# Penalty and maximum of the attention scores: one combined VectorE instruction per head in place of an addition and a reduction per eight heads

## What is computed

```
q, k, v = heads(norm(x) @ Wq.T + bq), heads(ctx @ Wk.T + bk), heads(ctx @ Wv.T + bv)
scores = einsum('bhqd,bhkd->bhqk', q / sqrt(16), k)
scores = scores + ((1.0 - attention_mask) * -10000.0)[:, None, :, :]
probs = softmax(scores, axis=-1)
x = x + tanh(g) * einsum('bhqk,bhkd->bhqd', probs, v)
```

## Time and profile before

| what | before |
|---|---|
| median of 3 runs | 851.88 us (849.93 to 851.89) |
| the profiled execution | 849.4 us |
| its span | 847.6 us |
| the attention stage's scores to exponentials | 481.5 to 613.7 us |

### The profile page before, as it was taken

How to read it: one execution, slowest core, us unless ns; L and a number is a source line. 1 busy time by engine, 2 the same in 40 slices (tenths; PEclk the granted TensorE clock), 3 DMA queues, 4 the chain that set the end, 5 groups by cost and what they waited for, 6 DMA issues and landing times.

```text
span 847.6 us, 15310 instructions
## 1 busy us (share of the span) xinstructions
PE 776.9 (92%) x5406; PEld 625.7 (74%) x5406; DVE 506.0 (60%) x1159; ACT 399.9 (47%) x817; POOL 227.0 (27%) x208
## 2 busy tenths in 40 slices
PE   8667899999999999999999789996789999999997
PEld 7466487788887888888887455654568878888886
DVE  5588875465583333343342897978766665756644
ACT  5598554244462222222223688778635344243222
POOL 0079210046501332232234166764300000000000
PEclk9989999999999999999999999999999999999999
DMA  8478740033242334443332600102004023050140
GB/s 303 143 263 300 279 169 1 1 126 125 99 164 69 63 63 70 78 79 63 68 45 31 221 13 27 63 2 75 2 2 102 1 51 76 1 126 0 27 100 26
DMA packets 37512, 74.47 MB, mean 88 GB/s; under 512 B 4448, under 2 KB 25568, under 8 KB 35680
## 3 DMA queue, kind: packets, MB, share of 16 engines
q1 hardware_dynamic: 30288, 64.16, 24.0%
q0 software_dynamic: 7152, 9.34, 6.4%
HBM read 59.76 MB, written 19.01 MB: 93 GB/s over the span
## 4 chain that ended last, share of the span: by engine, by line
PE 54%; DVE 16%; ACT 8%; DVEq 4%; issue 4%; DMA 2%; ACTq 0%; POOLq 0%; SPq 0%
PE t_y_ps L2281 8%; PE f_y L1775 4%; PE a_turned L999 3%; PE a_score L977 2%; ACT a_hhi L1165 2%; PE t_gate L2251 2%; PE a_score L978 2%; PE a_score L979 2%; PE t_up L2262 2%; PE t_up L2263 2%; PE t_up L2261 2%; PE t_gate L2252 2%; PE t_gate L2253 2%; PE a_proj L876 2%; PE t_h_turned L2270 2%
## 5 line engine op out<-in xcount | busy, mean ns | idle before, releaser
L2221 POOL DMA_INDIRECT sums<-t_y,t_dest x39 | 60.9, 1561 | 168.4 <-DMA sums<-t_y,t_dest 81.3
L2316 ACT CAST t_xT_hi<-t_x_turned 128x256 fp32r<-128x256 f32 x39 | 14.5, 372 | 139.2 <-PE t_x_turned L2242 139.2
L2281 PE MATMUL t_y_ps<-W,t_hidT 128*128 x312 | 73.8, 379 | 0.8 <-ACT t_hidT L2326 0.8
L1165 ACT CAST a_hhi<-a_hid 128x512 fp32r<-128x512 f32 x48 | 29.8, 620 | 87.5 <-DVEq L1450 85.9
L2281 PEld LDWEIGHTS t_y_ps<-W,t_hidT 128*128 128x128 f32 x312 | 59.1, 190 | 10.5 <-issue 1.0
L1452 DVE TENSOR_TENSOR a_hlo<-a_hid,a_hhi 128x512 fp32r<-128x512 f32 x48 | 33.2, 693 | 35.1 <-ACT a_hhi L1165 35.1
L1154 ACT ACTIVATE a_act_g<-a_score 128x512 f32<-128x512 f32 x48 | 28.6, 596 | 46.4 <-PE a_score L979 45.9
L2345 DVE TENSOR_TENSOR t_hid<-t_act_g,t_up 128x512 f32<-128x512 f32 x39 | 28.5, 731 | 35.9 <-ACT t_act_g L2321 32.6
L832 POOL TENSOR_TENSOR a_sc<-a_sc,a_nmx 128x512 f32<-128x512 f32 x32 | 33.3, 1042 | 55.8 <-DVE a_nmx L1298 55.8
L1114 ACT ACTIVATE a_pr<-a_sc,a_nmx 128x128 f32<-128x128 f32 x128 | 40.8, 390 | 14.3 <-DVE a_nmx L1298 13.5
L2356 DVE TENSOR_SCALAR t_y<-t_y_ps,t_dest 128x256 f32<-128x256 f32 x39 | 18.9, 484 | 38.3 <-PE t_y_ps L2281 38.3
(11 more groups left out here) (426 smaller groups left out, 2287.8 us busy)
## 6 DMA issues: line engine op xcount, KB each, us to landing
W<-in_w_dram SPq DMA_DIRECT2D x9, 1536.0 KB, 8.1
a_cb<-comb_rows SPq DMA_DIRECT2D x16, 512.0 KB, 8.2
W<-m_rows SPq DMA_DIRECT2D x14, 512.0 KB, 4.9
slot_tokens<-in_blank_rows_dram SPq DMA_DIRECT2D x1, 5031.0 KB, 20.5
t_x<-slot_tokens SPq DMA_DIRECT2D x39, 129.0 KB, 3.0
a_raw<-in_w_dram SPq DMA_DIRECT2D x3, 1536.0 KB, 6.7
X<-in_x_dram SPq DMA_DIRECT2D x4, 512.0 KB, 6.1
ctxT_all<-in_ctxT_dram SPq DMA_DIRECT2D x4, 512.0 KB, 8.7
```

Of the source, the lines that this page charges most:

```text
L1165: act.copy(hhi[u % 2][:], hid[u % 2]).then_inc(hhi_ready, 1)
L2221: pool.indirect_dma_start(sum_dram, bass.IndirectOffsetOnAxis(ap=dest[p][:, 0:1].bitcast(U32), axis=0), y[p][:], None, compute_op=ALU.add) ...
L2281: last = pe.matmul(y_ps[p][:, 0:D], hidT[p][:, h], W[:, ds(e, 1), at:at + D], start=(h == 0), stop=(h == HT - 1))
```

## The change

VectorE's `soft` becomes a loop over two groups of four heads. Each head is one `tensor_tensor_reduce`: it adds penalty and score, multiplies by -1 and writes the result to `sc`, and writes the smallest of the results to the head's column of `nmx`. The last of four signals `max_ready`, which now counts 4 a step, and `score_free` is gone: its waiters wait for the matching count of `max_ready`. The tile `sc` now holds the negated scores, so ScalarE's exponentials of groups 0 and 2 get a scale of -1, and POOL's `centre` subtracts `sc` from the broadcast `nmx`. The wait for old exponentials stands before each group in place of each half.

```diff
@@ block.sync
-                sp.wait_ge(score_free, 2 * CH * (c - 1))
+                sp.wait_ge(max_ready, 4 * CH * (c - 1))
@@ block.gpsimd, centre(s, g)
-                pool.wait_ge(max_ready, 2 * s + g // 2 + 1)
+                pool.wait_ge(max_ready, 4 * s + g + 1)
                 part = sc[s % 2][:, g]
-                pool.tensor_tensor(part, part, nmx[s % 2][:, g].rearrange("p (i o) -> p i o", o=1).broadcast_to([128, 4, 128]),
-                                   ALU.add).then_inc(centred_ready, 1)
+                pool.tensor_tensor(part, nmx[s % 2][:, g].rearrange("p (i o) -> p i o", o=1).broadcast_to([128, 4, 128]), part,
+                                   ALU.subtract).then_inc(centred_ready, 1)
@@ block.tensor, scores(s) and gate_up(u)
-                wait(pe, score_free, 2 * s)
+                wait(pe, max_ready, 4 * s)
...
-                    pe.wait_ge(score_free, 2 * B)
+                    pe.wait_ge(max_ready, 4 * B)
@@ block.scalar, exps(s, g)
-                    act.wait_ge(max_ready, 2 * s + g // 2 + 1)
+                    act.wait_ge(max_ready, 4 * s + g + 1)
                     for i in range(4):
-                        last = act.activation(pr[s % 2][:, g, i], sc[s % 2][:, g, i], ACT.Exp, bias=nmx[s % 2][:, g, i:i + 1])
+                        last = act.activation(pr[s % 2][:, g, i], sc[s % 2][:, g, i], ACT.Exp, bias=nmx[s % 2][:, g, i:i + 1],
+                                              scale=-1.0)
@@ block.vector, soft(s, half)
-                wait(dve, exp_ready, 4 * (s - 2) + 2 * half + 2)
-                part = sc[s % 2][:, 2 * half:2 * half + 2].rearrange("p r i t -> p (r i) t")
-                dve.tensor_tensor(part, score[:, half * 1024:(half + 1) * 1024].rearrange("p (h t) -> p h t", h=8),
-                                  pen[c % 2][:, j:j + 1].broadcast_to([128, 8, 128]), ALU.add).then_inc(score_free, 1)
-                dve.drain()
-                dve.tensor_reduce(nmx[s % 2][:, 2 * half:2 * half + 2].rearrange("p r i -> p (r i)"), part, AX.X, ALU.max,
-                                  negate=True).then_inc(max_ready, 1)
+                for r in (2 * half, 2 * half + 1):
+                    wait(dve, exp_ready, 4 * (s - 2) + r + 1)
+                    for i in range(4):
+                        last = dve.tensor_tensor_reduce(sc[s % 2][:, r, i], score[:, r * 512 + i * 128:r * 512 + (i + 1) * 128],
+                                                        pen[c % 2][:, j], -1.0, 3e38, ALU.add, ALU.min,
+                                                        nmx[s % 2][:, r, i:i + 1])
+                    last.then_inc(max_ready, 1)
```

More of the change, by code:

```diff
@@ L660, in attention_feed_forward @@
         proj_ready, kept_act, kept_dve, pen_ready = sem("proj_ready"), sem("kept_act"), sem("kept_dve"), sem("pen_ready")
-        score_ready, score_free, max_ready, exp_ready = sem("score_ready"), sem("score_free"), sem("max_ready"), sem("exp_ready")
+        score_ready, max_ready, exp_ready = sem("score_ready"), sem("max_ready"), sem("exp_ready")
         centred_ready = sem("centred_ready")
```

## The result

The changed kernel takes 844.02 us (median of 4 runs, 842.87 to 844.69), the kernel before 851.88 beside it (4 runs, 849.93 to 855.24): ratio 0.9888, 95% interval 0.9852 to 0.9924 (the two medians alone divide to 0.9908). The sign of the prediction holds. The gain is well over the 4.8 us forecast: 7.9 us by the medians, 9.5 by the ratio. The forecast's own range began at 844: the median is just inside it, while 851.9 x 0.9888 = 842.3 is outside, and just outside the wider range too, which began at 842.5. The profiled execution took 842.87 us with a span of 841.1.

The account below looks back on a forecast made before the run. The attention stage was taken as balanced, VectorE paying only where it is in the path. Terms: 1.4 + 0.5 + 1.0 + 2.2 - 0.3 = 4.8 us; 851.9 - 4.8 = 847.1 us; range 844 to 850.

Parts of the forecast that it names:

- the wider range: Total time: the 8 in 10 range, from 842.5 to 859 us.
- p = 0.275: VectorE's combined instructions: start-to-start pitch of 0.275 us, the maximum's write adding 0.075; a half 2.2 us, 0.24 less.
- rival 3: VectorE's combined instructions: the maximum comes for free, pitch 0.20, a half 1.6 us; 10.9 us gained, 841.0; chance 0.09.
- Rival 2: VectorE's combined instructions: no overlap, pitch 0.36, 6.7 us slower, 858.6; far end pitch 0.5, 883; chance 0.21 together.
- From 528 to 542: Within steps 5 to 9, VectorE fuller than TensorE: two of four halves counted, 2 x 0.24 = 0.5 us gained.
- steps 10 and 11: 561.7 to 579.7 us, VectorE doing one thing after another: four halves, 4 x 0.24 = 1.0 us gained.
- the late steps: Steps 12 to 15: 0.36 from exp 3 and 0.24 from the first half, three steps, plus 0.4: 2.2 us gained.
- gain 0.45 a step, it just fits: Steps 2 to 4: group 3's exponentials after 3.45 us instead of 3.9; three steps, 1.4 us gained.
- POOL's 9.17 of 10 leaves about 0.6 a step: Steps 2 to 4: POOL's busy share leaves about 0.6 us a step, enough for the 0.45 gain.
- The clock, left out of the sum: The lower granted clock after 580 us may move the time either way by a microsecond, held by the range.
- The later release of the score banks: Score banks freed by the last group's signal: steps 2 to 4 lose 0.3 us; covered in the full steps.

Follow-up runs that it names:

- the fourth of its traces: The changed kernel run again with no edit, as the control beside the reordering of POOL's queue: 842.84 us, ratio 0.9905 to the kernel before.
- the third: The changed kernel run again with no edit, as the zero for three variants beside it: 844.91 us, ratio 0.9893 to the kernel before.
- the two forms: The changed kernel with its signal per four heads, 847.22 us, and the same with one signal per half, 846.31 us.
- the old form with four signals: Kernel before, its addition and reduction split into four groups of 512 columns with a signal each: 859.39 us, ratio 1.0091.

## Why the prediction was right in sign and short in size

**The step that failed is the pitch, the term "p = 0.275" of "What takes its place".** The argument for it was half right. There is a second part, it lasts 0.083 us, and the Trainium skill's sentence ("VectorE: DVE Perf Modes", "Two Vector instructions with no wait between them") that an op that also writes its accumulator is two instructions agrees with the trace. The error was to add the part to the pitch instead of letting it run beside the next instruction. The pair of the earlier trace rows already showed it, with the line of the trace of before that stands between its two:

```profile
629.36 0.16 DVE L1405 MATCH_REPLACE8 a_oh<-a_largest,a_cur 128x16 f32<-128x16 f32 x1
```

The loads came 0.15 us apart while load and replacement last 0.09 and 0.16, so the replacement still ran when the next pair's load started. The pitch is 0.21, close to rival 3's 0.20, and rival 3 had been given 0.09. Rival 2 is refuted here: instructions of 0.286 and 0.083 us repeat every 0.21 us, and only where a drain was put in by hand did the pitch become 0.42.

The Trainium skill's rule that the next op doesn't start until the pipe is empty ("VectorE: DVE Perf Modes", "The DRAIN you can't avoid") does not hold for these instructions. The same section adds that a next op that isn't held starts earlier, which the prediction left out, and with that the trace agrees. The Trainium skill's advice not to fuse chained ops for speed and to keep the count of ops low (same page, "Rules for kernel authors") did not hold for this pair either: there are 448 more instructions, and the kernel is faster.

**With the measured pitch the forecast's own terms.** A half gets shorter by 2.44 - 1.69 = 0.75 us, not 0.24. From 528 to 542 two halves were counted: 1.5 us, and steps 5 to 9 gave 1.6. In steps 10 and 11 four halves would be 3.0, TensorE caps it as rival 3 said (2.0), and 1.8 came. In the late steps two halves and the wait were to count; 4.1 us for three steps and 1.0 in the last, 5.1 against 6.1 of rival 3. These terms were rightly placed, and too small because of the pitch. In the late steps the clock may have a share as well: the changed kernel took 23.2 us for steps 12 to 14 and 8.9 to the last exponential where the clock from 580 to 610 was 1.00 (the fourth of its traces), and 24.6 and 10.3 where it was 0.89 (the third), the level of before. Against before that is a gain of 5.8 or of 3.1 us.

**The early steps, "gain 0.45 a step, it just fits", failed on their own.** They gave nothing, although the half is shorter than forecast. The three steps were not alike at 7.0 us either, but 6.7, 7.0 and 8.2 by the starts of the scores. "POOL's 9.17 of 10 leaves about 0.6 a step" took a busy share for room. What counts is the order of POOL's queue: between the output's addition and the centring stands a weight piece of 0.83 + 1.00 us, which ends 1.1 us after the maximum is ready. Moving it, and nothing else, brought 1.4 us in those steps; in the kernel before it brings nothing in the time. Beside the short half the signal per four heads does nothing that can be measured: it only moves the wait to the centring, as the two forms' waits above show.

**That the time came out so near the range is luck.** With a pitch of 0.21 rival 3's sum, 841.0, was due. The early steps, which rival 3 counted at 1.8, gave nothing, and in the profiled execution the late start took back 3.4; neither was foreseen.

**The clock, left out of the sum, was worth a microsecond,** as much as the prediction allowed it either way. In both traces of before TensorE's granted clock was 0.66 in the 5 us after the last exponential, so most of them at the lower of its two levels (1.2 of 2.4 GHz), after steps in which TensorE idled 2.3 us before the values. After the change TensorE idles 1.6 us there and the clock was 1.00. What the clock cost there is seen in the lines: the same matmul of L979 lasts 0.63 us before and 0.39 after, and from the last exponential to the next `values` it is 6.7 us before and 5.2 after. From the last exponential to the end is 1.4 us less, in five traces 0.5 to 1.6. In the other kernels the clock in those 5 us went with the half too: 0.66 to 0.76 in all six traces with a half of 2.4 us or more, with 233.6 to 234.3 us to the end, and 1.00 in all fourteen with the short half, with 232.0 to 233.4. That the shorter idle time is what kept the clock up is argued, not shown.

**The later release of the score banks** showed as forecast: the scores wait for the maximum 7 times, 2.5 us in all, 0.8 of which the kernel before waited too. From 542 to 560, where TensorE is full, there is none, as was forecast. That it costs 0.3 us was not confirmed: with the wait per bank nothing was gained.

**What stays open.** The parts without the start add up to 9.9 us, and the medians say 7.9. Five traces of the changed kernel against two of before give 8.7 without the start. The stage began at 479.7, 479.9 and 483.8 in three traces with the old instructions, at 483.1 to 485.7 in five of the changed kernel. Without the reading of the maximum it was 481.0, and in the old form with four signals 482.3, which speaks for scatter of the stages before it, but so few traces don't settle why the changed kernel's are the late ones.

## What to carry to other kernels

A second part of an instruction that only writes a small result ran beside the next instruction here; price a chain by the distance of starts, and look for the smallest such distance among unlike instructions in the trace. An engine's busy share in a slice says nothing about when it gets to a job: look at what stands ahead of it in its queue at the moment at which the faster producer will be ready, and reorder that with the change. A finer signal takes away its own wait, but look at what the consumer waits for next: here 3.4 us of waiting for the maximum became waiting for the centring, and the time stayed.

## What the hardware showed that was not expected

- The read of the accumulator (83 ns) costs 0.01 us of pitch: 0.21 with it, 0.20 without. A 128x1 write behind it costs as little (0.22).
- An explicit drain behind a head costs 0.20 us of pitch (0.42 against 0.21): the overlap of 0.08 us is lost, and 0.12 us pass from the end of one head (500.02 + 0.29, and its read ends at 500.32) to the start of the next (500.44). Between the addition of 1024 elements at 504.52 and its reduction, the drain of before left 0.08:

```profile
505.82 1.22 DVE L1298 TENSOR_REDUCE a_nmx<-a_sc 128x8 f32<-128x1024 f32 x1
```

- Addition and reduction of 512 elements take 681 and 686 ns, of 1024 1216 and 1220: halving the size leaves 56% of the time.
